# Cross-attention block with a ternary FFN on one core: rows and probabilities transposed once as fp32, and split into fp16 halves on the way out of PSUM

## The reference, cut to what matters

```python
# x, ctx: (8, 1024, 512) fp32; w_q, w_k, w_v: (512, 512); W1: (2048, 512), W2: (512, 2048)
def xattn(query, key, value):
    q, k, v = query @ w_q, key @ w_k, value @ w_v
    scores = where(tril, q @ k.T / sqrt(512), -inf)
    return softmax(scores) @ v
def ternary(w):
    scale = max(mean(abs(w)), 1e-8)
    return clip(round(w / scale), -1, 1)
def ffn(x):
    return gelu(x @ ternary(W1).T + b1) @ ternary(W2).T + b2
x = x + tanh(g_xattn) * xattn(layernorm(x), ctx, ctx)
x = x + tanh(g_ffn) * ffn(layernorm(x))
```

## Time and profile before

| | |
|---|---|
| time, median of 3 runs | 1773.13 us (1772.98 to 1773.37) |
| profiled execution, first to last instruction | 1771.6 us |
| PE busy | 1716.0 us (97%) |
| DVE busy | 903.2 us (51%) |
| ACT busy | 784.0 us (44%) |
| POOL busy | 307.7 us (17%) |
| mean granted clock of TensorE | 0.990 |

### The profile page before, as it was taken

How to read it: one execution, slowest core, us unless ns; L and a number is a source line. 1 busy time by engine, 2 the same in 40 slices (tenths; PEclk the granted TensorE clock), 3 DMA queues, 4 the chain that set the end, 5 groups by cost and what they waited for, 6 DMA issues and landing times.

```text
span 1771.6 us, 27014 instructions
## 1 busy us (share of the span) xinstructions
PE 1716.0 (97%) x10048; PEld 911.8 (51%) x10048; DVE 903.2 (51%) x1639; ACT 784.0 (44%) x1160; POOL 307.7 (17%) x341
## 2 busy tenths in 40 slices
PE   5799999999999999889999999999999999999999
PEld 2466656665666666555444444444444444444444
DVE  4565666666656665778443343334334434344332
ACT  2334343433343345433445544454545544554443
POOL 1111111111111111122111211122112211121110
PEclk8899999999999999999999999999999999999999
DMA  4112121121212144332110011101110111101100
GB/s 172 60 49 84 49 90 43 53 91 36 97 48 91 41 137 150 106 134 94 37 48 25 23 47 47 47 0 47 47 47 0 47 47 47 34 13 47 48 25 24
DMA packets 44570, 105.17 MB, mean 59 GB/s; under 512 B 5328, under 2 KB 5328, under 8 KB 43344
## 3 DMA queue, kind: packets, MB, share of 16 engines
q1 hardware_dynamic: 43920, 103.83, 17.5%
q10 hardware_dynamic: 576, 0.27, 0.1%
HBM read 70.53 MB, written 33.55 MB: 59 GB/s over the span
## 4 chain that ended last, share of the span: by engine, by line
PE 81%; DVE 9%; issue 7%; ACT 1%; DMA 1%; POOL 1%; DVEq 0%; SPq 0%; POOLq 0%; ACTq 0%
PE t_ps L842 12%; PE pT_ps L948 12%; PE s_ps L948 12%; PE v_ps L842 11%; PE o_ps L906 8%; PE s_ps L870 7%; PE v_ps L919 7%; PE t_ps L888 7%; PE xT_ps L831 3%; DVE v_s L797 2%; PE pT_ps L855 1%; DVE w_s L745 1%; DVE negmax L661 1%; DVE pT L652 1%; DVE ctx_s L545 1%
## 5 line engine op out<-in xcount | busy, mean ns | idle before, releaser
L771 DVE SCALAR_TENSOR_TENSOR v_s<-g,sc,v_s 128x512 f16<-128x512 f32 x256 | 233.3, 912 | 508.5 <-ACT v_s L492 506.0
L948 PE MATMUL pT_ps<-w_s,v_s 128*128 128x512 f16 x1024 | 265.5, 379 | 0.8
L948 PE MATMUL s_ps<-w_s,v_s 128*128 128x512 f16 x1024 | 262.8, 379 | 0.0
L842 PE MATMUL v_ps<-ctx_s,w_s 128*128 128x512 f16 x1024 | 241.9, 379 | 0.9 <-DVE w_s L745 0.9
L842 PE MATMUL t_ps<-ctx_s,w_s 128*128 128x512 f16 x1024 | 241.9, 379 | 0.0
L906 PE MATMUL o_ps<-v_s,pT 128*128 128x512 f16 x864 | 198.6, 381 | 9.5 <-DVE pT L652 9.5
L888 PE MATMUL t_ps<-xnT,a_s 128*128 128x256 f16 x1536 | 183.4, 277 | 23.1 <-ACT a_s L475 11.5
L870 PE MATMUL s_ps<-ctx_s,tT 128*128 128x512 f16 (+3 forms) x1152 | 197.6, 326 | 0.1
L492 ACT ACTIVATE v_s<-g,sc 128x512 f16<-128x512 f32 x256 | 184.8, 722 | 8.4
L919 PE MATMUL v_ps<-wv_s,ctx_s 128*128 128x512 f16 x768 | 178.7, 383 | 7.8 <-DVE ctx_s L545 7.8
L888 PEld LDWEIGHTS t_ps<-xnT,a_s 128*128 128x128 f16 x1536 | 151.9, 100 | 49.2 <-issue 14.4
(11 more groups left out here) (99 smaller groups left out, 1654.2 us busy)
## 6 DMA issues: line engine op xcount, KB each, us to landing
x_ring<-in_x SPq DMA_DIRECT2D x64, 256.0 KB, 2.9
raw<-in_ctxT SPq DMA_DIRECT2D x8, 2048.0 KB, 8.2
out_y<-x_ring SPq DMA_DIRECT2D x64, 256.0 KB, 3.0
raw<-out_y SPq DMA_DIRECT2D x64, 256.0 KB, 3.2
out_y<-v_s SPq DMA_DIRECT2D x64, 256.0 KB, 2.1
w_in<-in_w1T SPq DMA_DIRECT2D x16, 512.0 KB, 5.0
w_in<-in_w2T SPq DMA_DIRECT2D x16, 512.0 KB, 5.0
ctx_s<-in_wqT SPq DMA_DIRECT2D x4, 256.0 KB, 6.5
```

The costliest lines, as they stand in the source:

```text
L771: v.scalar_tensor_tensor(out=g_s[:, f % 4, LO], in0=g32[:, f % 2], scalar=col(C_SG), in1=g_s[:, f % 4, HI], op0=ALU.mult, op1=ALU.subtract ...
L842: last_mm = mm(h_ps[f % 2], w1_s[:, c, (f % FC) * P:(f % FC + 1) * P], yT[:, (f // FC) % 2, a, c, :], start=(a == HI and c == 0), stop=(a ...
L948: last_mm = mm(y_ps[i], g_s[:, f % 4, a, i * P:(i + 1) * P], w2_s[:, f, :], start=(f == 0 and a == HI), stop=(f == FC - 1 and a == LO))
```

## The change

The fp32 tiles `xn32` and `p32` are transposed themselves, one transpose for each 128x128 block instead of two, into fp32 PSUM tiles of the same number of bytes. `xn_s` and `p_s` and the four instructions that made them are gone. The halves are made when PSUM is read: ACT writes HI with a copy (`rows_upper`, `probs_upper`), and DVE writes LO as PSUM minus HI (`rows_lower`, and the LO of `pT`). So each of the two ways out of PSUM, one instruction before, is an ACT instruction and then a DVE instruction. POOL has only the reciprocal root of the row left of the row's work.

In TensorE's stream the transposes stand between matmuls: block j of the probabilities behind the j-th scores matmul, and the four blocks of a row ahead of the last four V matmuls, or in the FFN ahead of each pair of output matmuls of the chunks 4, 6, 9 and 12. Where a slot has no scores or no V matmuls left, they stand in a run.

On DVE the LO half of `pT` comes behind the row statistics, where the copy stood ahead of them; the LO half of the transposed row comes behind the LO half of V and ahead of the context work.

```diff
-            def transposes(k, r):
-                pe.wait_ge(xn_lo, k + 1)
+            def transpose_row(k, r, c):
+                if c == 0:
+                    pe.wait_ge(xn_ready, k + 1)
+                    if not isinstance(k, int) or k > 0:
+                        pe.wait_ge(xT_ready, k)
+                tr = nc.tensor.transpose(xT_ps[:, c], xn32[:, r, c * P:(c + 1) * P], ident[:, :])
+                if c == DC - 1:
+                    tr.then_inc(x_tr, 1)
...
                                 last_mm = mm(s_ps[:, lo:hi], tT[:, pr, ta, c, q * P:(q + 1) * P],
                                              ctx_s[:, par, ca, c, lo:hi], start=(n == 0 and c == 0),
                                              stop=(n == 2 and c == DC - 1))
+                                if scored < n_tr:
+                                    transpose_probs(scored)
+                                scored += 1
                     last_mm.then_inc(s_mm, 1)
+                for j in range(scored, n_tr):
+                    transpose_probs(j)
...
                         for c in range(DC):
+                            if n == 2 and rows:
+                                transpose_row(t + XT_LEAD, (s + XT_LEAD) % 2, c)
                             last_mm = mm(v_ps[:, :], ctx_s[:, par, ca, c, j * P:(j + 1) * P], wv_s[:, va, c, :],
...
+                        if rows:
+                            nth = XT_STEPS.index(f)
+                            transpose_row(NT + GT + g * GT + nth, nth % 2, i)
                         for a in (HI, LO):
                             last_mm = mm(y_ps[i], g_s[:, f % 4, a, i * P:(i + 1) * P], w2_s[:, f, :],
...
+            def probs_upper(t, s):
+
+                w = ((s - 1) % TB + 1) * P
                 act.wait_ge(p_tr, t)
-                a.activation(p_s[:, HI, 0:w], p32[:, 0:w], ACT.Copy, scale=P_UP).then_inc(p_hi, 1)
+                a.activation(pT[:, HI, 0:w], pT_ps[:, 0:w], ACT.Copy, scale=P_UP).then_inc(pT_hi, 1)
+
+            def rows_upper(k, dst):
+
+                act.wait_ge(x_tr, k + 1)
+                a.activation(dst, xT_ps[:, :, :], ACT.Copy).then_inc(xT_hi, 1)
...
+            def rows_lower(k, upper, lower):
+
+                dve.wait_ge(xT_hi, k + 1)
+                v.tensor_tensor(lower, xT_ps[:, :, :], upper, ALU.subtract).then_inc(xT_ready, 1)
...
-                    dve.wait_ge(p_tr, t)
-                    v.tensor_copy(pT[:, :, 0:w], pT_ps[:, :, 0:w]).then_inc(pT_ready, 1)
                 if norm:
                     v.bn_stats(bn6[:, rk], src).then_inc(bn_done, 1)
+                if s >= 1:
+
+                    w = ((s - 1) % TB + 1) * P
+                    dve.wait_ge(pT_hi, t)
+                    v.scalar_tensor_tensor(out=pT[:, LO, 0:w], in0=pT_ps[:, 0:w], scalar=P_UP, in1=pT[:, HI, 0:w],
+                                           op0=ALU.mult, op1=ALU.subtract).then_inc(pT_ready, 1)
```

More of the change, by code:

```diff
@@ L217, in w_dst, with row_dst @@
             return dst[:, :, :].rearrange("p a n -> p (a n)")[:, k * WCH:(k + 1) * WCH]
+        def row_dst(t, s, last, half):
+            if not last or t + XT_LEAD < NT:
+                pr, q = ((s + XT_LEAD) // 2) % 2, (s + XT_LEAD) % 2
+                return xnT[:, pr, half, :, q * P:(q + 1) * P]
+            u = t + XT_LEAD - NT
+            return yT[:, 0, half, :, u * P:(u + 1) * P]
         LN_STEPS = (2, 4, 7, 10)
@@ L456, in slot @@
                 if s >= -XT_LEAD and (not last or t + XT_LEAD < NT + GT):
[L457 to L464, removed]
+                    rows_upper(t + XT_LEAD, row_dst(t, s, last, HI))
                 for m, n in w_turn(t, "S") if last else ():
@@ L498, in group @@
                         hidden(F + 2, f + 2)
[L499 to L504, removed]
                     if f in XT_STEPS and (not last or F + FC < NG * FC):
                         i = XT_STEPS.index(f)
[L507 to L510, removed]
+                        rows_upper(NT + GT + (it * 2 + gg) * GT + i, yT[:, (gg + 1) % 2, HI, :, i * P:(i + 1) * P])
             hidden(0, 0)
@@ L585, in scale_product @@
             def scale_product():
-                for n, half in enumerate((s_ps[:, :], pT32)):
+                for n, half in enumerate((s_ps[:, :], pT_ps[:, :])):
                     dve.wait_ge(a_mm, n + 1)
@@ L707, in slot @@
                                            op1=ALU.subtract).then_inc(v_split, 1)
+                if s >= -XT_LEAD and (not last or t + XT_LEAD < NT + GT):
+                    rows_lower(t + XT_LEAD, row_dst(t, s, last, HI), row_dst(t, s, last, LO))
                 if s > 0 and (not last or t + TB < NT):
@@ L908, in slot @@
                     last_mm.then_inc(pv_mm, 1)
+                rows = s >= -XT_LEAD and (not last or t + XT_LEAD < NT + GT)
                 if s >= -1 and (not last or t + 1 < NT):
@@ L921, in slot @@
                     last_mm.then_inc(v_mm, 1)
-                if s >= -XT_LEAD and (not last or t + XT_LEAD < NT + GT):
-                    transposes(t + XT_LEAD, (s + XT_LEAD) % 2)
+                elif rows:
+                    for c in range(DC):
+                        transpose_row(t + XT_LEAD, (s + XT_LEAD) % 2, c)
             for s in range(FIRST_SLOT, 1):
@@ L943, in group @@
                     pe.wait_ge(g_split, F + 1)
+                    rows = f in XT_STEPS and (not last or F + FC < NG * FC)
                     for i in range(GT):
@@ L951, in group @@
                             last_mm.then_inc(y_mm, 1)
-                    if f in XT_STEPS and (not last or F + FC < NG * FC):
-                        i = XT_STEPS.index(f)
-                        transposes(NT + GT + g * GT + i, i % 2)
             with pe.Fori(0, NG // 2 - 1) as it:
```

80 lines of the change are left out of this document (28 added, 52 removed).

## The result

The changed kernel takes 1763.16 us (median of 4 runs, 1762.19 to 1766.49), the kernel before 1773.25 us beside it. The ratio is 0.9939, with a 95% interval of 0.9923 to 0.9956: 10 us faster, where the forecast was 25 us, or 1748. The direction and the range held; the size did not, and most of what was gained came from a place that the prediction had costed at nothing or as a loss.

What follows compares the result with a forecast made beforehand. TensorE was taken as the bound, busy 1716.0 of 1771.6 us; 40.3 us saved there less waits of 6.2, 4.0 and 4.6 left 25.5, so 1748 us, range 1737 to 1790.

Steps and rivals of the forecast that it cites:

- I take 0.056, because the row of the same operation is nearer than the row of the same type: TensorE's stream: each of 800 fp32 transposes priced at 0.056 us, the pitch of the fp16 ones.
- TensorE's own sum: Transposes on TensorE: 89.4 less 44.7 gives 44.7 us saved; 40.3 after fp32 loads and the start.
- rival 3: TensorE's fp32 transposes take four passes, 0.215 us each, so the kernel takes 1864 us; chance 0.08.
- 4× faster for FP32: Skill rule on TensorE's transpose mode: a quarter of the doubled fp32 matmul's 0.215, so 0.054 us, supporting the forecast.
- rival 2: An fp32 transpose on TensorE streams at two cycles a column, 0.107 us; slower, 1784 us; chance 0.22.
- POOL loses the LO passes and nothing waits for it more: POOL's queue: dropping its LO passes over the rows was costed at nothing.
- 2.3 us for each of the two reductions: Last batch, behind POOL's two reductions: the row's LO half on DVE comes 2.3 us later, 4.6 us lost.
- Rival 5: DVE becomes the bound oftener, so the waits double to 29.6 us and the time is 1762; chance 0.09.
- The fp32 loads: Stationary loads sticking out behind 128-column matmuls in slot 0 and the last slot: 64 x 0.054, 3.5 us lost.
- The two waits: TensorE waits at `o_ps` for DVE's LO of `pT`: 0.89 us in seven slots 0, 0.57 in seven slots 2.
- ACT's moved HI passes: HI pass over the probabilities, moved to the slot's head beside TensorE's scores; costed at nothing, up to 1.2 us if uncovered.
- DVE's new pass in the FFN: LO pass of 0.69 us for 60 rows, within 506 us of DVE idle time: nothing; 41 us if uncovered.

Runs made afterwards that it cites:

- before_no_reduction: The kernel before, with the last batch's two cross-partition reductions of the weights' sums replaced by an add of each partition's own sum: 1759.82 us, ratio 0.9924.
- after_no_reduction: The changed kernel, with the last batch's two cross-partition reductions of the weights' sums replaced by an add of each partition's own sum: 1757.64 us, ratio 0.9911.
- probs_only: Half of the change on the kernel before: only probabilities transposed as fp32, rows as before with POOL's LO pass: 1769.86 us, ratio 0.9982.
- reduction_first: The kernel before, with POOL's cross-partition reduction moved ahead of the rows' LO pass in the two slots that sum weights' totals: 1767.45 us, ratio 0.9972.
- fp16_twice: The kernel before, with each fp16 transpose of half a row tile in the FFN made twice (480 more): 1800.41 us.
- pool_pass: The changed kernel, with an unread POOL pass over the normalised row put where its LO pass stood in the attention part: 1782.64 us, ratio 1.0062.
- rows_only: Half of the change on the kernel before: only rows transposed as fp32, probabilities as before in fp16 halves: 1768.86 us, ratio 0.9979.

## Why the prediction was wrong, step by step

**The step that failed** is "I take 0.056, because the row of the same operation is nearer than the row of the same type". It is 0.109 us, in the FFN, in the attention part and in runs. The price was the neighbour's in type and not in operation: the trace's fp32 matmul, per record, taken over 128 columns, gave 0.107. With it TensorE's own sum is 2.2 us and not 44.7. It decides over the forecast: 42 us of it. That the time still fell, as forecast, is luck: the saving that was to bring it is 2 us, and another, which the sum had as a loss, stood in for it. The doubling into two records, which made rival 3, does not happen for a transpose. The rule of the Trainium skill that the prediction weighed ("4× faster for FP32", TensorE: Matmul & The Clock Gate, section Terms) would have given 0.054 by the prediction's estimate; measured is half of the doubled matmul's 0.215, so twice as fast and not four times, if that is the base that the rule means.

**A second term of the wrong size and sign** kept the time from rival 2's 1784. The prediction wrote that "POOL loses the LO passes and nothing waits for it more", and it charged 2.3 us for each of the two reductions. Slot 54 gained 6.4 us instead, and slot 60 1.2, which is hardly more than it varies by. The queue of POOL had been read for what it computes and not for what stands idle in front of it; the wait of 8.34 us for POOL's `rstd` was among the rows shown, and its cause was not followed one instruction further up. A reading was off as well: ACT's copy in the earlier trace rows starts at 714.78 and ends at 715.79, where the prediction has it done at 714.78. `before_no_reduction` against `after_no_reduction` puts 8 of the 10 us measured on the two reductions together with the pass ahead of them. Rival 5 had named 1762, within 1.2 us of the result, for a doubling of the waits; it did not happen, and the nearness is chance.

**The fp32 loads**, 3.5 us, are not paid. A load is recorded at 141 ns, and behind a matmul of 128 columns the next one still starts 0.056 us later. A transpose in slot 0 costs 0.115, so only 0.006 us more than elsewhere (with 0.056 of its neighbour the pairs are 0.17 us apart). That slot's TensorE sum of 8 x 0.110 was nearly right for a wrong reason: a stream of 0.056 with a load of 0.054 on top, where the stream alone is the whole.

**The two waits were right.** `o_ps` started 5.09 and 5.28 us behind V where 5.06 and 5.25 were forecast, so DVE's chain, its order and its passes had been read well. Against what TensorE needs with the measured transposes (4.63 - 1.34 + 8 x 0.115 = 4.21, and 5.24 - 0.67 + 2 x 0.11 = 4.79) they are waits of 0.88 and 0.49 us, against 0.89 and 0.57. Slots 3 to 7 show none, as forecast.

**Costed at nothing, and nothing**: ACT's moved HI passes, and DVE's new pass in the FFN, where DVE still waits 500.8 us for ACT. The FFN did not get 13 us shorter but 0.2, by the price of a transpose alone.

**The start** is POOL's too, as far as its passes go: the first V matmul begins at 54.5 to 55.9 us in the six kernels that have a POOL pass over the row (before, `probs_only`, `reduction_first`, `before_no_reduction`, `fp16_twice`, `pool_pass`) and at 51.2 to 52.7 in the eight that have none. The reduction `call<-cmax` there moved up from 51.25 to 48.58.

**What stays open**: why the loop ends gain 1.5 us. Slots 17 and 33 together take 18.2 to 18.9 us in the five kernels that transpose the rows as fp16, 17.9 in `rows_only`, and 16.1 to 16.8 in the eight that transpose both as fp32, `pool_pass` among them, so it is not POOL's pass. Open too are 2.6 of the 3.5 us of slots 1 and 5, which `pool_pass` does not give back, and why slot 53 grows when only the probabilities change. No run was made for these.

## What to carry to other kernels

Where two halves of a split are transposed, transposing the fp32 once costs TensorE the same; what such a change brought here lay in the passes that it took off the other engines, so look for who stands behind those. Read an engine with little work for its order, and not its busy share: follow a wait to the instruction it names, and that one to what it waited for. When a pass out of PSUM becomes two, put the earlier half's source first in TensorE's order and the pass that TensorE needs first in DVE's; here that was worth more than the change itself.

## What the chip showed that I had not expected

- A transpose of 128 x 128 fp32 takes 0.109 us of TensorE's stream, once, and 0.056 in fp16; its fp32 load of 141 ns adds at most 0.006 us even behind a matmul of 0.056 us.
- DVE's pass over two SBUF tiles of 128x512 takes 0.75 us, and took 1.64 with 1.1 us of a POOL pass beside it; the ternary pass of 1.28 us took 2.28 so.
- A reduction across partitions on POOL, mostly 0.40 us long itself, occupies it for 14 to 17 us: for the two of the last batch, in both kernels, 5.83 to 7.80 us ahead and 6.98 to 9.76 us behind, which no instruction of the trace shows. A pass of 1.04 us that nobody reads, put into every slot, cost the changed kernel 19.5 us, most of it in slots behind such reductions.
